# A one-core network of two mixing layers: order of stores, loads and projections in attention, and the values' rest on GpSimd

## The chip, the cores and the metric

The kernel runs on one core of a Trainium2 chip. The metric is the device time of one execution in microseconds, as the median of several executions. Engines are named as in the profile: PE is TensorE's matmul, PEld its weight load, DVE is VectorE, ACT is ScalarE, POOL is GpSimd, SP is SyncE, which here only issues DMAs.

## The reference, cut to what matters

Two layers on an input of 4 x 1024 x 256, each layer a mixing part and a feed-forward part with adaptive layer norms. The change touches only the second layer's attention:

```python
q = (h @ Wq).reshape(b, s, 16, 64).transpose(0, 2, 1, 3)
k = (h @ Wk).reshape(b, s, 4, 64).transpose(0, 2, 1, 3)
v = (h @ Wv).reshape(b, s, 4, 64).transpose(0, 2, 1, 3)
q, k = _apply_rope(q, cos, sin), _apply_rope(k, cos, sin)
scores = jnp.einsum('bkgqd,bkpd->bkgqp', q.reshape(b, 4, 4, s, 64), k) * scale
scores = jnp.where(causal, scores, -1e30)
out = jnp.einsum('bkgqp,bkpd->bkgqd', softmax(scores), v)
```

The rest is a long convolution by spectra, a feed-forward with binarized weights, and a mixture of two of eight experts.

## The kernel before

One loop of four turns, one for each batch element, runs on all engines; each engine's program is written out by hand in `before.py`, and semaphores tie them. A turn is: convolution part, feed-forward, attention (norm, projections, 16 heads), output projection, experts. float32 precision comes from splitting an operand into a high part (rounded to fp32r) and a low part (the rest), so a product costs three matmuls.

**Attention's opening.** `project(k, col)` on TensorE makes two blocks of 128 columns of queries or keys for one half of the 1024 rows: k = 0, 2 are the keys, 1, 3 the queries of heads 0 to 3, and 4 to 9 those of heads 4 to 15, two halves each. VectorE's `rotate(k)` multiplies each block by sine and cosine into `turned(k)`, a part of the tile `oT`; `rotate` on GpSimd (or `turn_and_add` on VectorE for k = 1, 3) adds them up; ScalarE's `high(k)` copies the high part, VectorE's `low(k)` subtracts for the low part (semaphore `rope_lo`). `project_values(h)` makes the values of one half; ScalarE's `value_rows(h)` copies their high part to `vhi` and VectorE's `value_low(h)` subtracts, from PSUM, into `vlo`. TensorE's order is: project 0, 1, values of half 0, norm, project 2, 3, the eight row scores of head 0 (`score_rows`), values of half 1, `turn_maxima(0)`, project 4, then the heads. All PSUM banks are handed out in turn by `Banks.take`; a taker waits for the last user of its bank.

**A head.** For head u the loop runs over 12 blocks n = 0 to 11 of (column half c, row tile j), `BLOCKS`. In each, TensorE makes the transposed scores of the block (`score_cols`: two matmuls, and on a diagonal block a third that adds the mask from `causal`), ScalarE takes the exponential twice (`exps`: full precision and high part), VectorE or GpSimd subtracts for the low part (`score_low`), and four blocks later TensorE multiplies with the values (`values`, three matmuls). The softmax's maxima come from a second set of scores, with query rows in partitions: `rows_at(u, n)` places the rows 0 to 3 of head u + 2 at blocks 8 to 11 and rows 4 to 7 of head u + 1 at blocks 0 to 3; VectorE reduces each (`row_maxima`). At block 6 the maxima of head u + 1 are turned over by TensorE (`turn_maxima`) and copied by ScalarE to `nmr`. Projections 5 to 9 stand at block 4 of heads 0, 3, 4, 7 and 8 (`PROJECT_AT`), their high and low parts at later blocks (`HIGH_AT`, `LOW_AT`). All have one buffer, `hrow`, so `high(k)` waits for the store of k - 1.

**SP's queue.** SP issues in order and waits in order. Its turn for head u (lines 1506 to 1534) waits for the exponentials of head u - 1, then loads the low queries of u + 1 (`load_query_low`) and the queries of u + 2 (`load_query`, tile `qhh`, three buffers) from the DRAM tensor `q_scratch`, at every fourth head the next keys, then the sums of head u - 1 (`load_sums`, 4 KB), the maxima of u + 1 (`load_maxima`), and the inverse of the sums through DRAM and back (`spread_inverse`, which waits for VectorE's reciprocal at block 9 and for its own store). Last, in heads 0, 1, 3, 4, 7 and 8 (`STORE_IN`), it waits for `rope_lo` and stores the turned queries of projection k, 1 MB, to `q_scratch`; where k is odd it then waits until both halves have landed.

TensorE's `score_rows(u, 0)` waits for `q_loaded(u)`, line 507 in the profile is its matmul.

Of the kernel before, what the change touches and what calls it, by code (L numbers as in the profile page):

```python
# [53 lines left out]
HIGH_AT = {(0, 7): 4, (1, 5): 5, (3, 9): 6, (4, 9): 7, (7, 9): 8, (8, 9): 9}  # L54
LOW_AT = {(0, 10): 4, (1, 8): 5, (3, 11): 6, (4, 11): 7, (7, 11): 8, (8, 11): 9}
STORE_IN = {0: 4, 1: 5, 3: 6, 4: 7, 7: 8, 8: 9}
# [55 lines left out]
def adaln_hyena_binffn_gqa_moe(nc, d, out, gate_scratch, kf_scratch, q_scratch, k_scratch, inverse_scratch, scratch):  # L112
    es = ExitStack()
    with es:
# [117 lines left out]
        def turned(k):  # L232

            n = k if k < 4 else 2 + k % 2
            return oT[:, 2 * n:2 * n + 2, :].rearrange("p a n -> p (a n)").rearrange("p (k n) -> p k n", n=HALF)
# [17 lines left out]
        def full(n):  # L253

            r = n % FRING
            return pT[:, r, :] if r < FRING - 1 else mix[:, 4:6, :].rearrange("p k n -> p (k n)")

        def stored_at(k):

            if k in (0, 2):  # L260
# [20 lines left out]
                 "m_loaded1", "v_high",  # L281
# [94 lines left out]
        def _(pe):  # L376
# [106 lines left out]
            def project_values(h):  # L483

                for t in range(4 * h, 4 * h + 4, 2):
                    b = bk.take(pe, ("v", t), until=(s["v_done"], t // 2 + 1))
# [124 lines left out]
            with pe.Fori(0, B):  # L611
# [43 lines left out]
                project(3, QCOL)  # L655
                for i in range(NT):
                    score_rows(0, i)
                project_values(1)
                turn_maxima(0)
                project(4, QCOL + GQ * HD)  # L660
# [66 lines left out]
        def _(act):  # L727
# [61 lines left out]
            def exps(u, c, j):  # L789
# [3 lines left out]
                if n == 0:  # L793
                    act.wait_ge(s["rest_stored0"], 16 * 2)
                    act.wait_ge(s["next_loaded"], 16 * 3)
                if n >= PRING:
# [30 lines left out]
            def value_rows(h):  # L827
                for t in range(4 * h, 4 * h + 4, 2):
                    b = bk.wait(act, ("v", t))
                    A(vhi[:, :, t:t + 2, 0:HD].rearrange("p g t n -> p t g n"),  # L830
                      ps[:, b, :].rearrange("p (t g n) -> p t g n", t=2, g=KV), ACT.Copy).then_inc(s["v_high"], 1)
# [7 lines left out]
            with act.Fori(0, B):  # L839
# [28 lines left out]
                for h in range(NHALF):  # L868
# [6 lines left out]
                    store_rest(2 * h + 1)  # L875
                value_rows(1)
                turn_maxima(0)
# [27 lines left out]
        def _(dve):  # L905
# [164 lines left out]
            def value_low(h):  # L1070

                for t in range(4 * h, 4 * h + 4, 2):
                    dve.wait_ge(s["v_high"], t // 2 + 1)
                    b = bk.wait(dve, ("v", t))
                    V.tensor_tensor(vlo[:, :, t:t + 2, 0:HD].rearrange("p g t n -> p t g n"),
                                    ps[:, b, :].rearrange("p (t g n) -> p t g n", t=2, g=KV),
                                    vhi[:, :, t:t + 2, 0:HD].rearrange("p g t n -> p t g n").bitcast(F32),
                                    ALU.subtract).then_inc(s["v_done"], 1)

# [28 lines left out]
            with dve.Fori(0, B) as bi:  # L1108
# [91 lines left out]
                value_low(0)  # L1200
# [3 lines left out]
                value_low(1)  # L1204
# [421 lines left out]
```

## Time and profile before

| | |
|---|---|
| median of 3 runs | 2111.86 us (2111.76 to 2113.53) |
| the profiled execution | 2106.92 us, span 2105.0 us |
| mean granted TensorE clock | 0.924 |
| PE busy | 1805.4 us, 86% |
| DVE busy | 1534.3 us, 73% |
| ACT busy | 987.6 us, 47% |
| POOL busy | 716.6 us, 34% |
| chain that ended last | PE 56%, DVE 19%, DMA 7%, issue 6% |

The profile is one execution on the chip. Times are microseconds from the start of the span. "Idle before" is the time an engine stood still before an instruction, with the one whose end released it. The granted clock is the share of the full 2.4 GHz at which TensorE was let run: 1.00 or, at the lower of its two levels, 0.50; a stretch that holds both has a mean between. Attention's 16 heads lie between about 262 and 516 us in the first turn, and again in each of the other three.

### The profile page before, as it was taken

Reading aid. Unit: us, or ns where it says so; the run is one execution under the profiler, and the core shown is the slowest. Engines: PE = TensorE matmul, PEld = TensorE weight load, DVE = VectorE, ACT = ScalarE, POOL = GpSimd, SP = SyncE. Lnnn points to the kernel's source line nnn. Section 1 sums busy time; section 2 is a strip of 40 time slices with the busy share of each in tenths; the row PEclk is TensorE's granted clock in tenths of the full one; section 3 lists DMA queues with packets and bytes.
Section 4 is the critical chain, followed back from the end, with each engine's and each line's share of the span. In section 5 each row is a group of like instructions: output and inputs, shape, how many; then the busy total and the mean of one; then the engine's idle time right before and its main releaser. Section 6 shows DMA issues by size and latency. Waiting matters only on the chain.

```text
span 2105.0 us, 27381 instructions
## 1 busy us (share of the span) xinstructions
PE 1805.4 (86%) x9108; PEld 1451.2 (69%) x9108; DVE 1534.3 (73%) x2774; ACT 987.6 (47%) x2113; POOL 716.6 (34%) x747
## 2 busy tenths in 40 slices
PE   6868799999875889999977778999987687999997
PEld 3747677778764767778765567777776576777885
DVE  4588878875658887777448887777654978778745
ACT  1303266776320446667431326667722033666742
POOL 0051144533224234444115214444411513444321
PEclk8988899999987989999989889999998898999998
DMA  6500334431410053443150034433241004344305
GB/s 237 191 1 1 104 101 112 106 87 47 180 51 1 1 149 101 103 116 72 32 215 0 1 82 114 116 96 86 52 180 62 0 1 120 96 116 117 81 27 200
DMA packets 92184, 187.14 MB, mean 89 GB/s; under 512 B 29119, under 2 KB 44287, under 8 KB 88326
## 3 DMA queue, kind: packets, MB, share of 16 engines
q1 hardware_dynamic: 84742, 171.66, 27.9%
q10 hardware_dynamic: 7296, 13.63, 2.3%
q8 instruction: 80, 1.31, 0.3%
q14 instruction: 66, 0.54, 0.1%
HBM read 129.39 MB, written 45.89 MB: 83 GB/s over the span
## 4 chain that ended last, share of the span: by engine, by line
PE 56%; DVE 19%; DMA 7%; issue 6%; DVEq 5%; ACT 3%; POOL 2%; SPq 1%; POOLq 1%; ACTq 0%
PE ps L384 8%; PE ps L507 6%; PE ps L679 5%; PE ps L527 5%; PE ps L550 5%; PE ps L547 5%; PE ps L548 5%; PE ps L529 5%; PE ps L390 3%; PE ps L720 3%; DMA qhh<-q_scratch 2%; DVE hrow L978 2%; DMA q_scratch<-hrow 2%; DVE psplit L1083 2%; DVE ps L1063 2%
## 5 line engine op out<-in xcount | busy, mean ns | idle before, releaser
L1308 POOL TENSOR_TENSOR psplit<-pT,psplit 128x384 fp32r<-128x384 f32 (+3 forms) x320 | 303.7, 961 | 547.2 <-ACT psplit L801 543.7
L1063 DVE CUSTOM_DVE_ANT_0 ps<-ps,mrow 128x128 f32<-128x128 f32 (+7 forms) x512 | 385.3, 766 | 132.8 <-PE ps L507 131.8
L801 ACT ACTIVATE psplit<-ps 128x512 fp32r<-128x512 f32 (+3 forms) x768 | 373.0, 486 | 0.0
L800 ACT ACTIVATE pT<-ps 128x512 f32<-128x512 f32 (+3 forms) x512 | 256.5, 501 | 214.4 <-PE ps L533 135.4
L507 PE MATMUL ps<-khl,qhh 128*128 128x512 f32 (+3 forms) x768 | 253.0, 392 | 76.0 <-DMA qhh<-q_scratch 26.3
L527 PE MATMUL ps<-qhh,khl 128*128 128x512 f32 (+3 forms) x768 | 272.8, 355 | 0.4
L529 PE MATMUL ps<-q,k 65*128 65x512 f32 (+3 forms) x768 | 269.3, 351 | 0.0
L547 PE MATMUL ps<-psplit,vhi 128*65 128x512 f32 (+3 forms) x768 | 267.9, 349 | 0.0
L550 PE MATMUL ps<-psplit,vhi 128*65 128x512 f32 (+3 forms) x768 | 262.9, 342 | 0.0
L548 PE MATMUL ps<-psplit,vlo 128*65 128x512 f32 (+3 forms) x768 | 262.3, 341 | 0.0
L759 ACT ACTIVATE work<-ps,modb 128x512 f32<-128x512 f32 x48 | 37.3, 777 | 400.6 <-PE ps L462 400.6
L507 PEld LDWEIGHTS ps<-khl,qhh 128*128 128x128 f32 x768 | 132.4, 201 | 99.3 <-issue 51.4
L527 PEld LDWEIGHTS ps<-qhh,khl 128*128 128x128 f32 x768 | 146.7, 191 | 51.6 <-DVE mx L1063 4.9
L1275 POOL TENSOR_TENSOR rstd<-var,neghalf 128x4 f32<-128x4 f32 x34 | 34.5, 1015 | 430.3 <-DVE var L975 430.3
L1083 DVE TENSOR_TENSOR psplit<-pT,psplit 128x512 fp32r<-128x512 f32 x192 | 131.2, 708 | 48.7 <-ACT psplit L801 47.9
L529 PEld LDWEIGHTS ps<-q,k 65*128 65x128 f32 x768 | 147.1, 192 | 17.4
L800 ACT ACTIVATE mix<-ps 128x512 f32<-128x512 f32 (+2 forms) x256 | 117.9, 461 | 84.3 <-PE ps L529 49.9
L384 PE MATMUL ps<-hT,wqkv 128*128 128x512 f32 x480 | 127.9, 422 | 19.0 <-DVE hT L987 19.0
L550 PEld LDWEIGHTS ps<-psplit,vhi 128*65 128x65 f32 x768 | 106.0, 138 | 44.3 <-issue 3.0
L1083 DVE TENSOR_TENSOR psplit<-mix,psplit 128x512 fp32r<-128x512 f32 x128 | 99.2, 775 | 42.8 <-ACT psplit L801 42.8
L548 PEld LDWEIGHTS ps<-psplit,vlo 128*65 128x65 f32 x768 | 106.2, 138 | 34.8
L1094 DVE TENSOR_TENSOR oT<-work,mix 64x1024 f32<-64x1024 f32 x64 | 94.3, 1474 | 45.5 <-DMA mix<-inverse_scratch 44.6
(176 smaller groups left out, 3505.7 us busy)
## 6 DMA issues: line engine op xcount, KB each, us to landing
qhh<-q_scratch SPq DMA_DIRECT2D x112, 256.0 KB, 4.9
q_scratch<-hrow SPq DMA_DIRECT2D x24, 1024.0 KB, 5.4
mix<-inverse_scratch SPq DMA_DIRECT2D x64, 256.0 KB, 3.5
q<-q_scratch SPq DMA_DIRECT2D x56, 256.0 KB, 4.3
sgn<-sgn_scratch SPq DMA_DIRECT2D x8, 1024.0 KB, 13.3
Kf<-kf_scratch SPq DMA_DIRECT2D x4, 2048.0 KB, 17.5
khl<-k_scratch SPq DMA_DIRECT2D x24, 256.0 KB, 6.5
in_w<-in_w_scratch SPq DMA_DIRECT2D x4, 1536.0 KB, 10.5
```

Of the source, the lines that this page charges most:

```text
L384: i = mm(o, lhs(a, q), rhs(c, q), start=n == 0, stop=n == len(pairs) - 1)
L507: q = mm(ps[:, b + c // HALF, 0:e - c], qhh[:, r, i * P:(i + 1) * P], khl[:, g % 2, c:e], start=True, stop=True)
L527: mm(ps[:, b, 0:hi - lo], khl[:, g % 2, j * P:(j + 1) * P], qhh[:, r, lo:hi], start=True, stop=False)
L529: i = mm(ps[:, b, 0:hi - lo], k2[:, g % 2, j * P:(j + 1) * P], q2[:, u % 2, lo:hi], start=False, stop=not diagonal)
L547: mm(o, vhi[:, g, j, :], high, start=j == 0, stop=False)
L548: mm(o, vlo[:, g, j, :], high, start=False, stop=False)
L550: mm(o, vhi[:, g, j, :], low, start=False, stop=j == 4 * c + 3).then_inc(s["pv_done"], 1)
L800: A(full(n)[:, 0:hi - lo], ps[:, b, 0:hi - lo], ACT.Exp, scale=SCALE)
L801: A(psplit[:, n % PRING, 0, 0:hi - lo], ps[:, b, 0:hi - lo], ACT.Exp, scale=SCALE)\
L1063: V.tensor_tensor_reduce(out=v, in0=v, in1=mrow[:, L - n:L], scale=1.0, scalar=-3e38, op0=ALU.add, op1=ALU.max, accum_out=mx[:, u % 2, i:i ...
L1083: V.tensor_tensor(psplit[:, n % PRING, 1, 0:m], full(n)[:, 0:m], psplit[:, n % PRING, 0, 0:m].bitcast(F32), ALU.subtract)\
L1308: G.tensor_tensor(psplit[:, n % PRING, 1, 0:m], full(n)[:, 0:m], psplit[:, n % PRING, 0, 0:m].bitcast(F32), ALU.subtract)\
```

## The change

- SP: the loads of head u's turn are no longer behind the wait for the store's landing. Stores 6 to 9 go right behind `load_query` in heads 4, 5, 8 and 9 (`STORE_FIRST`); stores 4 and 5 stay at the end of heads 0 and 1 (`STORE_LATE`) without a wait behind them. The wait for both halves stands ahead of the `load_query` that is the first to read them, in heads 2, 6 and 10.
- High and low parts of projections 4 and 5 come at earlier blocks.
- TensorE: project 4 goes ahead of head 0's row scores, `turn_maxima(0)` ahead of the values of half 1. `turned(4)` lies where `turned(1)` was.
- Values: ScalarE copies them twice, the high part and all of it (`vfull`, in room of `pT` and `oT`); GpSimd subtracts. The bank is free after ScalarE's copies. The first two exponentials wait for GpSimd, as they write that room. VectorE's `value_low` is gone, and rotates 4 where it stood.
- ScalarE: the values of half 1 come behind the copy of head 0's maxima. GpSimd: `rotate(0)` comes ahead of its fills, then the values' low parts of half 0, `rotate(2)`, `rotate(4)`, the low parts of half 1.

```diff
-HIGH_AT = {(0, 7): 4, (1, 5): 5, (3, 9): 6, (4, 9): 7, (7, 9): 8, (8, 9): 9}
-LOW_AT = {(0, 10): 4, (1, 8): 5, (3, 11): 6, (4, 11): 7, (7, 11): 8, (8, 11): 9}
-STORE_IN = {0: 4, 1: 5, 3: 6, 4: 7, 7: 8, 8: 9}
+HIGH_AT = {(0, 4): 4, (1, 2): 5, (3, 9): 6, (4, 9): 7, (7, 9): 8, (8, 9): 9}
+LOW_AT = {(0, 6): 4, (1, 5): 5, (3, 11): 6, (4, 11): 7, (7, 11): 8, (8, 11): 9}
+STORE_LATE = {0: 4, 1: 5}
+STORE_FIRST = {4: 6, 5: 7, 8: 8, 9: 9}
...
-            n = k if k < 4 else 2 + k % 2
+            n = k if k < 4 else 1 if k == 4 else 2 + k % 2
...
+        def vfull(t):
+
+            return pT[:, t // 2, :] if t < 4 else oT[:, 0, (t - 4) * D:(t - 2) * D]
...
                 project(2, KCOL)
                 project(3, QCOL)
+                project(4, QCOL + GQ * HD)
                 for i in range(NT):
                     score_rows(0, i)
+                turn_maxima(0)
                 project_values(1)
-                turn_maxima(0)
-                project(4, QCOL + GQ * HD)
...
+                if n < 2:
+                    act.wait_ge(s["v_done"], n + 1)
...
-                      ps[:, b, :].rearrange("p (t g n) -> p t g n", t=2, g=KV), ACT.Copy).then_inc(s["v_high"], 1)
+                      ps[:, b, :].rearrange("p (t g n) -> p t g n", t=2, g=KV), ACT.Copy)
+                    A(vfull(t), ps[:, b, :], ACT.Copy).then_inc(s["v_copied"], 1)
...
+                turn_maxima(0)
+                act.wait_ge(s["rope_lo"], 1)
                 value_rows(1)
-                turn_maxima(0)
...
-                value_low(0)
+                rotate(4)
                 for i in range(NT):
                     row_maxima(0, i)
                 negate(0)
-                value_low(1)
-                rotate(4)
...
+            def value_low(h):
+
+                for t in range(4 * h, 4 * h + 4, 2):
+                    pool.wait_ge(s["v_copied"], t // 2 + 1)
+                    G.tensor_tensor(vlo[:, :, t:t + 2, 0:HD].rearrange("p g t n -> p t g n"),
+                                    vfull(t).rearrange("p (t g n) -> p t g n", t=2, g=KV),
+                                    vhi[:, :, t:t + 2, 0:HD].rearrange("p g t n -> p t g n").bitcast(F32),
+                                    ALU.subtract).then_inc(s["v_done"], 1)
...
+                rotate(0)
                 G.memset(vhi[:, :, :, HD:HD + 1].bitcast(F32), 1.0)
...
-                for k in (0, 2):
-                    rotate(k)
+                value_low(0)
+                rotate(2)
+                rotate(4)
+                value_low(1)
...
                     if u + 2 < HEADS:
+                        if u and (u + 2) % GQ == 0:
+                            for k in (2 * g + 4, 2 * g + 5):
+                                sp.wait_ge(*rope_stored(k))
                         load_query(u + 2)
+                    if u in STORE_FIRST:
+                        store(STORE_FIRST[u])
...
-                    if u in STORE_IN:
-                        store(STORE_IN[u])
-                        if STORE_IN[u] % 2:
-                            for k in (STORE_IN[u] - 1, STORE_IN[u]):
-                                sp.wait_ge(*rope_stored(k))
+                    if u in STORE_LATE:
+                        store(STORE_LATE[u])
```

## Rows read from the trace of the kernel before

**Rows 1.** Windows between copies of the maxima: length, busy by engine, clock, DMA.

```profile
core 0: us, PE busy (x) PEld busy (x) DVE busy (x) ACT busy (x) POOL busy (x), PEclk, DMA share, GB/s
303.68:325.46 21.78, 18.39 (x94) 14.53 (x93) 13.50 (x26) 11.21 (x29) 7.47 (x9) 0.92 0.34 76
342.99:357.95 14.96, 14.49 (x85) 11.45 (x84) 13.44 (x27) 11.88 (x30) 8.25 (x8) 1.00 0.46 137
357.95:376.71 18.76, 15.79 (x83) 12.23 (x81) 11.29 (x25) 11.02 (x28) 5.64 (x7) 0.91 0.36 82
376.71:393.32 16.61, 16.61 (x94) 13.29 (x93) 13.20 (x26) 10.94 (x29) 7.37 (x9) 1.00 0.28 65
425.91:443.09 17.18, 14.25 (x83) 11.22 (x82) 11.29 (x25) 11.03 (x29) 5.61 (x7) 1.00 0.41 87
443.09:457.14 14.05, 14.05 (x83) 11.22 (x82) 10.76 (x25) 10.76 (x28) 5.57 (x7) 1.00 0.34 77
928.76:947.46 18.70, 15.85 (x83) 12.52 (x82) 11.29 (x25) 11.03 (x28) 5.64 (x7) 0.91 0.36 81
1815.74:1837.41 21.67, 18.41 (x94) 14.53 (x93) 13.49 (x26) 11.21 (x29) 7.48 (x9) 0.92 0.32 75
1869.98:1888.81 18.83, 15.80 (x83) 12.27 (x82) 11.30 (x25) 11.03 (x29) 5.61 (x7) 0.91 0.35 82
1938.01:1955.20 17.19, 14.26 (x83) 11.22 (x82) 11.29 (x25) 11.03 (x29) 5.62 (x7) 1.00 0.41 89
```

**Rows 2.** Timeline from 348 to 362: start, duration, engine, line, operation, idle before.

```profile
348.72 0.31 ACT L801 ACTIVATE psplit<-ps 128x128 fp32r<-128x128 f32 x1
...
349.52 0.49 SPq L1494 DMA_DIRECT2D mix<-inverse_scratch  x1
...
350.62 0.58 SPq L1454 DMA_DIRECT2D q_scratch<-hrow  x1
...
355.41 0.53 SPq L1473 DMA_DIRECT2D q<-q_scratch  x1
...
355.99 1.24 SPq L1468 DMA_DIRECT2D qhh<-q_scratch  x2
...
361.35 0.30 PE L507 MATMUL ps<-khl,qhh 128*128 128x128 f32 x1 [2.97 <-DMA qhh<-q_scratch]
```

**Rows 3.** Timeline from 290 to 312, heads 1 and 2.

```profile
292.30 1.22 DVE L1056 TENSOR_TENSOR hrow<-oT,hrow 128x1024 fp32r<-128x1024 f32 x1
...
295.94 0.60 SPq L1454 DMA_DIRECT2D q_scratch<-hrow  x1
...
302.06 1.24 SPq L1468 DMA_DIRECT2D qhh<-q_scratch  x2
...
307.55 0.30 PE L507 MATMUL ps<-khl,qhh 128*128 128x128 f32 x1 [3.39 <-issue]
```

**Rows 4.** Timeline from 248 to 263, attention's opening.

```profile
248.21 1.93 PE L507 MATMUL ps<-khl,qhh 128*128 128x128 f32 x4 [5.75 <-DVE vlo L1075]
...
254.11 4.27 PE L384 MATMUL ps<-wqkv,hT 128*128 128x256 f32 x24
...
256.13 0.17 DVE L1068 TENSOR_SCALAR nm<-mx 128x8 f32<-128x8 f32 x1
...
258.24 3.05 PE L384 MATMUL ps<-hT,wqkv 128*128 128x512 f32 x12
...
259.18 1.28 ACT L800 ACT_TABLE_LOAD   x1
259.93 1.22 DVE L1042 TENSOR_TENSOR oT<-ps,rope 128x1024 f32<-128x1024 f32 x1 [0.18 <-PE ps L384]
...
262.04 0.60 ACT L800 ACTIVATE pT<-ps 128x512 f32<-128x512 f32 x1 [1.58 <-PE ps L533]
```

**Rows 5.** Groups by form, 262 to 516: count, busy us, mean ns, idle before.

```profile
L1056 DVE TENSOR_TENSOR hrow<-oT,hrow 128x1024 fp32r<-128x1024 f32 x6 | 8.7, 1457 | 0.0
...
L1308 POOL TENSOR_TENSOR psplit<-pT,psplit 128x512 fp32r<-128x512 f32 x16 | 20.7, 1291 | 32.0 <-ACT psplit L801 32.0
```

**Rows 6.** Loads of the sums, tile `den`: from issue to landing, all 64.

```profile
DMA to landing us min/median/max: 1.9/2.0/7.5
```

More of the change, by code:

```diff
@@ L280, in adaln_hyena_binffn_gqa_moe @@
                  "q_loaded1", "q_loaded2", "q2_loaded0", "q2_loaded1", "k_loaded0", "k_loaded1", "v_done", "nm_done", "nmr_done", "m_loaded0",
-                 "m_loaded1", "v_high",
+                 "m_loaded1", "v_copied",
                  "exp_done", "causal_made", "low_pool", "low_dve", "pv_done", "o_done", "sum_loaded", "inverse_done",
@@ L485, in project_values @@
                 for t in range(4 * h, 4 * h + 4, 2):
-                    b = bk.take(pe, ("v", t), until=(s["v_done"], t // 2 + 1))
+                    b = bk.take(pe, ("v", t), until=(s["v_copied"], t // 2 + 1))
                     for u in range(2):
@@ L1068, in negate @@
                 V.tensor_scalar(nm[:, u % 2, :], mx[:, u % 2, :], -1.0, None, ALU.mult).then_inc(s["nm_done"], 1)
[L1070 to L1078, printed above, removed]
             def score_low(u, c, j):
@@ L1367, in _ @@
                             score_low(u, c, j)
-                        if (u, n) == (0, 3):
-                            rotate(4)
                         if (u, n) in PROJECT_AT:
```

## The prediction

> **What bounds the kernel now.** I read the windows of attention first, cut from one copy of the negated row maxima to the next (the copy stands at block 6 of each head), so that each stretch is one head's length. A head at its best takes 14.05 us and TensorE is busy in all of it, VectorE for 10.76, ScalarE for 10.76, GpSimd for 5.57 [rows 1]. A head that also carries one query projection takes 16.61, again with TensorE busy throughout. So attention is bound by TensorE, and whatever makes TensorE idle is paid in full. The next thing to look for is which heads are longer than 14.05 or 16.61. Three a batch are much longer: the stretch of 21.78 (one projection in it), the one of 18.76, and the one of 17.18 to 18.94 [rows 1]. In all three the timeline shows TensorE standing still for about 3 us before the first row score of a head two ahead, and ended by the landing of that head's queries [rows 2, 3]. In most of them the granted clock of the stretch is then 0.91 or 0.92 instead of 1.00, with TensorE busy 15.79 us for work that takes 14.05 elsewhere [rows 1]: the stall also costs a piece at the lower level. Last comes the opening, read in the timeline.
>
> **Loads of queries no longer behind the store, heads 5 and 9.** Before, SP issues the store of turned queries at 350.62, waits for it to land, and only at 355.41 and 355.99 issues the loads of head 6's low parts and head 7's queries; TensorE waits 2.97 us for the latter, until 361.35 [rows 2]. The last exponential of head 4 starts at 348.72 and SP is through with the inverse at 349.52 + 0.49, so in the changed order the low load goes at about 350.1, the queries at 350.7, and the store behind them at about 352. They took at most 361.35 - 355.99 = 5.36 us to arrive; from 350.7 that is 356.1, and TensorE asks for them at 361.35 - 2.97 = 358.4. The stall goes, with 2.3 us to spare. What is late next is nothing: VectorE had 11.29 us of work in that stretch. Worth, against 14.05: the stretch of head 5 is 18.76 in the first batch and 18.83 in the fourth (four such, the two between read 19.02 and 18.81), 19.2 us in all; that of head 9 is 17.18, 18.70, 18.94 and 17.19, 15.8 us in all [rows 1]. Sum **-35.0**. Bounds: all of it, or -28 if each of the eight stretches stays 0.9 us long, as the one from 342.99 is.
>
> **Head 2.** Here the load of head 4's queries needs the store of k = 5 itself, so the wait stays; it only moves behind the low load. Before: low part made at 292.30 (1.22 us), store 295.94, loads 302.06, TensorE waits 3.39 until 307.55 [rows 3]. After: that low part is made at block 5 instead of 8, where VectorE has room, so the reciprocal, the inverse's store and its load, on which SP is blocked ahead of this store, come about 0.9 earlier; and the low load of 0.54 is no longer ahead of the queries' load. That makes the load some 1.6 us earlier and its flight perhaps 0.4 shorter. The stall falls from 3.4 to about 1.4. Whether the clock then stays up has no row for a gap of that length in this place; the stretch from 342.99, whose waits are short, stays at 1.00, those of head 2 at 0.92 [rows 1]. The stretch exceeds 16.61 by 5.17 to 5.06 (first and fourth batch, of four; 20.8 us in all). Of each I take 2.0 of stall and 1.7 of the clock, **-14.8**. Bounds: -2.4 (only 0.6 a batch and a clock as before) and -20.8.
>
> **Store behind the loads, heads 4 and 8.** The store issued just ahead of head 6's and 10's loads now follows them. The stretch of 14.96 us is 0.9 over a clean head [rows 1]; of that I take the part which is waiting for queries, 0.7 for the two heads of a batch, **-2.7**. Bounds: 0 and -7.5.
>
> **The opening.** Three moves at once. Project 4 (12 matmuls, 3.05 us) leaves the place between the maxima and head 0 and goes ahead of the first row scores, where TensorE idles: they began at 248.21 after 5.75 us of waiting [rows 4]. Worth nothing there, as the scores of the second four rows wait for a DMA that does not come earlier. The values' 24 matmuls (4.27 us) had lain beside VectorE's maxima; they now follow the turned maxima and lie beside the maxima's own DMA. So 4.27 in place of 3.05 stands behind the negation of 256.13. VectorE gains and loses about equally ahead of it (the low values' two subtractions out, two rotations of 1.22 in, partly beside waiting): +0.4. ScalarE makes two copies per pair of tiles rather than one (four more a batch, 0.60 each as I take them from an exponential of the same shape), and those of the last two pairs come behind the maxima's copy, and the table load of 1.28 behind them. Followed step by step: negation 256.5, values end about 261.5, copies 262.6, table load 263.9, first exponential 263.9 in place of 262.04. The first row score of head 1 waits for the same copies and comes at 262.6, as before. The third block of head 0 takes the bank that the first pair of exponentials (two of 0.60) frees, at about 265.1 in place of 263.2, and the row scores behind it wait. I take +1.5 a batch, **+6.0**; bounds -4 (the values run at full clock and ScalarE's extra copies hide) and +12. The values of the first half cost ScalarE two more copies ahead of the norm's second half, some 0.3 us, inside that. GpSimd's four subtractions at about 1.29 each take the place of VectorE's; they end near 264.4, before the first low part is asked for, so nothing. The waits of the first two exponentials on them are long met.
>
> On the table load the trace has 1.28 us and its engine idle after it [rows 4]. The Trainium skill (ScalarE: Activation LUTs, What ACT_TABLE_LOAD costs) counts a drain of about the same length on top, 2.66 us in all. That speaks against the change: by it the first exponential would come another 1.4 us later and the sum be about 5.5 us worse. No row shows the drain.
>
> **The sum.** -35.0 - 14.8 - 2.7 + 6.0 = -46.5. The profiled execution took 2106.92 (span 2105.0), the timed runs have their median at 2111.86, so 4.9 us above it, about what two or three more stretches at the lower clock make. I set the change on the median: 2111.86 - 46.5 = **2065.4** (2060.4 on the profiled one's footing).
>
> **The rivals.**
> A, *small gain*: head 2 keeps its stall and its low clock (-2.4) and the opening costs its bound (+12). With -35 for heads 5 and 9 and -1 for heads 4 and 8 that is -26: 2085. For it: store and load in series remain. Against: the wait shrinks by SP's order alone.
> B, *GpSimd in VectorE's way*: the subtractions of the first values (two of 1.29) fall beside VectorE's own low parts of the first half, which have two operands in SBUF. That form takes 1.22 where GpSimd is still and has a mean of 1.46 over six in attention [rows 3, 5]. Priced at two blocked lengths, 2.6, less the 1.25 VectorE waits for TensorE just after, it is +1.3 a batch: 2071. The Trainium skill (SBUF - State Buffer, on the shared port pair) says that the second of two such operations waits for the whole first one; the mean of 1.46 agrees in part. It lies inside the range.
> C, *slower than before*: the 1 MB store, now issued behind the loads, lies ahead of the 4 KB row of sums. That row lands in 2.0 us at the median but 7.5 at worst [rows 6]. Issued some 5 us into the head, about 355.6, and landing 7.5 later, it would be there at 363.1, while VectorE asks for it near 359.2; VectorE, in order, holds the row maxima behind its reciprocal, TensorE stands 3.9 us and loses another 1.6 at the lower clock. At four heads of four batches that is 16 x 5.5 = 88 against 46.5 won: 2153. It decides the sign once it costs over 2.9 us a head. Against: the store had landed 4.8 us after its issue [rows 2], so from 352 it is done at about 357.
> D, *it does not do what it says*: the query loads are held by something else (the exponentials of the head before), the stall of heads 5 and 9 stays by two thirds; -12 - 5 + 6: 2101. Against: the exponential at 348.72.
>
> **How the numbers follow.** Forecast with B inside it 0.68 (2050 to 2078), A 0.18, D 0.05, C 0.03, a gain above the forecast's own range 0.06. The range for 8 in 10 goes from 2050 to 2086: it takes in the forecast and most of A. About 0.2% (4.2 us) is what a measurement of this kernel can tell from no change: faster 0.94 (all but C and some of D), same 0.02 and slower 0.04 (C, and D with the opening at its bound).
>
> **What would show it.** The stretches of heads 5 and 9 at 14.05 to 14.3 with the clock at 1.00; the query load of head 7 issued before the store; the one of head 2 near 18 to 19; heads 4 and 8 at 14.3 to 14.7; the first exponential 1 to 3 us later after the negation than 5.9. It is wrong if a stretch of heads 5 or 9 stays above 16, if VectorE waits at the reciprocal, or if TensorE stands still ahead of head 0's third block for over 3 us.

## The result, and the profile after

| | before | after |
|---|---|---|
| median | 2112.63 us (2111.76 to 2113.53, 4 runs) | 2074.87 us (2071.98 to 2080.39, 4 runs) |
| the profiled execution | 2106.92, span 2105.0 | 2071.98, span 2070.2 |
| chain that ended last | PE 56%, DVE 19%, DMA 7% | PE 61%, DVE 17%, DMA 2% |

The ratio is 0.9824, interval [0.9802, 0.9847]: 37.8 us faster on the medians, 34.8 on the spans of the profiled executions. The forecast was 2065.4, with 2050 to 2086 around it. The direction held and the time is in the range; of the 46.5 us forecast, about 35 to 38 came. The profiled execution of after is the fastest of its four runs, and what is read from its trace is that one's.

I cut the trace of every kernel in the same way. The marks of a turn are VectorE's first normalised row of attention's norm, the negation of head 0's maxima, and ScalarE's copies of the maxima of head 1, 2 and so on, which delimit the heads as in [rows 1]. A stretch has the name of the head in whose block 6 it begins, so head 2's, the 21.78 of [rows 1], runs from the copy of head 3's maxima to that of head 4's. The one called "head 1", here and in the expectations, is an exception: it is the stretch from the copy of head 1's maxima to that of head 2's, from block 6 of head 0 to block 6 of head 1. What lies between two marks is compared turn by turn. Means over the four turns, in us; the last line is what one turn of after differs from before:

| | norm row to negation | negation to copy of head 1's maxima | "head 1" | head 2 | head 5 | head 9 |
|---|---|---|---|---|---|---|
| before | 31.23 | 17.76 | 15.45 | 21.81 | 18.86 | 18.00 |
| after | 33.22 | 18.99 | 14.44 | 19.61 | 14.05 | 14.07 |
| difference | +1.99 | +1.23 | -1.01 | -2.20 | -4.81 | -3.93 |

The other heads agree within 0.1. Times four that is +8.0 +4.9 -4.0 -8.8 -19.2 -15.7 = -34.8, which is the whole of what the spans differ by: outside attention both kernels spend 1004.2 to 1004.3 us.

The windows of after. Columns: stretch and its length, busy time of each engine (instructions), TensorE's granted clock, DMA share, GB/s. The first is head 2 in the first turn, the second head 2 in the second turn, then heads 4, 5 and 9 of the first:

```profile
307.09:327.21 20.12, 18.40 (x94) 14.41 (x93) 13.50 (x26) 11.22 (x29) 7.50 (x9) 0.92 0.26 63
802.04:820.35 18.31, 16.84 (x94) 13.27 (x93) 13.50 (x26) 11.21 (x28) 7.46 (x9) 1.00 0.30 65
344.74:359.79 15.05, 14.83 (x85) 11.46 (x84) 13.14 (x27) 11.67 (x30) 8.70 (x8) 1.00 0.55 143
359.79:373.85 14.06, 14.06 (x83) 11.22 (x82) 11.02 (x25) 10.79 (x29) 5.56 (x7) 1.00 0.37 87
423.05:437.12 14.07, 14.07 (x83) 11.20 (x82) 11.02 (x25) 10.78 (x28) 5.58 (x7) 1.00 0.39 85
```

Where [rows 1] had 18.76 for head 5 and 17.18 to 18.94 for head 9, there is now a clean head: TensorE busy all of it, clock 1.00. SP's queue around it, in the timeline (start, duration):

```profile
351.83 0.60 SPq L1480 DMA_DIRECT2D q<-q_scratch  x1
352.47 1.24 SPq L1475 DMA_DIRECT2D qhh<-q_scratch  x2
353.75 0.60 SPq L1461 DMA_DIRECT2D q_scratch<-hrow  x1
358.02 0.51 SPq L1491 DMA_DIRECT2D den<-work  x1
```

The two loads are issued first and the store behind them; in [rows 2] the store came first and the loads 4.8 us after it. Head 2, in contrast, still has a stall and, in three turns of four, still loses clock: TensorE is busy 18.40 in the first line above for the work that takes it 16.84 in the second.

### The profile page after: what moved, and what is told of

Its sections match the earlier page's. It is cut to its first block, busy times and chain, and to the rows that moved or that the text cites. A ratio compares the mean times of both kernels' runs of the same rounds, so it can differ in the third digit from the quotient of the medians.

```text
span 2070.2 us, 27393 instructions
## 1 busy us (share of the span) xinstructions
PE 1795.0 (87%) x9108; PEld 1441.8 (70%) x9108; DVE 1520.4 (73%) x2758; ACT 994.4 (48%) x2129; POOL 735.9 (36%) x763
## 4 chain that ended last, share of the span: by engine, by line
PE 61%; DVE 17%; ACT 5%; DVEq 5%; issue 5%; POOL 3%; DMA 2%; ACTq 1%; SPq 1%; POOLq 0%
PE ps L389 8%; PE ps L512 7%; PE ps L532 6%; PE ps L534 6%; PE ps L555 5%; PE ps L552 5%; PE ps L553 5%; PE ps L684 5%; PE ps L395 5%; PE ps L725 3%; DMA gate_scratch<-grow 2%; DVE prod L1140 2%; PE ps L538 2%; DVE ps L1072 1%; DVE oT L1093 1%
## 5 line engine op out<-in xcount | busy, mean ns | idle before, releaser
L552 PE MATMUL ps<-psplit,vhi 128*65 128x512 f32 (+3 forms) x768 | 265.2, 345 | 0.0
L555 PE MATMUL ps<-psplit,vhi 128*65 128x512 f32 (+3 forms) x768 | 259.7, 338 | 0.0
L389 PEld LDWEIGHTS ps<-hT,wqkv 128*128 128x128 f32 x480 | 98.0, 206 | 48.6 <-DVE hT L996 24.7
## 6 DMA issues: line engine op xcount, KB each, us to landing
Kf<-kf_scratch SPq DMA_DIRECT2D x4, 2048.0 KB, 17.5
```

The source lines that it names most:

```text
L389: i = mm(o, lhs(a, q), rhs(c, q), start=n == 0, stop=n == len(pairs) - 1)
L552: mm(o, vhi[:, g, j, :], high, start=j == 0, stop=False)
L555: mm(o, vhi[:, g, j, :], low, start=False, stop=j == 4 * c + 3).then_inc(s["pv_done"], 1)
```

## The experiments

A time is the median of the kernel's runs, and the ratio is to the kernel before, measured beside it on the same chip. Two kernels have one run each and no interval. Each stretch below is read from one profiled execution, of four turns.

### SP's order alone

The kernel before, with only SP's order changed as in the change:

```diff
-STORE_IN = {0: 4, 1: 5, 3: 6, 4: 7, 7: 8, 8: 9}
+STORE_LATE = {0: 4, 1: 5}
+STORE_FIRST = {4: 6, 5: 7, 8: 8, 9: 9}
...
+                        if u and (u + 2) % GQ == 0:
+                            for k in (2 * g + 4, 2 * g + 5):
+                                sp.wait_ge(*rope_stored(k))
...
+                    if u in STORE_FIRST:
+                        store(STORE_FIRST[u])
```

> The kernel before with SP's new order alone (stores behind the loads, the wait for landing ahead of the load that needs it); opening, high and low parts as before. Theory 1 (SP's order is the whole gain, the opening costs about 5 us net): the stretches of heads 5 and 9 fall to 14.05 (35 us), head 2's stretch of 21.8 loses about 0.6 us a batch; heads 0 and 1 keep 15.13 and 15.45; 2074 to 2077. Rival (the gain needs the earlier parts or the other opening too): heads 5 or 9 stay above 16, 2085 or more.

Measured: 2070.62 (2065.89 to 2072.47), ratio 0.9796 [0.978, 0.9812], below the 2074 to 2077 expected. Heads 5 and 9 are 14.05 and 14.07 in the mean, as in after. "Head 1" is as before (15.44), head 2 only a little shorter (20.91 for 21.81). So the part of the change that touches SP alone is worth all that the whole change is, on fewer edits: the opening and the earlier parts together add nothing. The windows of "head 1" and head 2 in the first turn:

```profile
275.77:291.20 15.43, 14.96 (x86) 11.58 (x84) 12.72 (x24) 12.53 (x30) 7.99 (x8) 1.00 0.45 121
305.31:325.98 20.67, 18.45 (x94) 14.38 (x93) 13.51 (x26) 11.21 (x29) 7.47 (x9) 0.92 0.29 71
```

### The same with the earlier high and low parts

```diff
-HIGH_AT = {(0, 7): 4, (1, 5): 5, (3, 9): 6, (4, 9): 7, (7, 9): 8, (8, 9): 9}
-LOW_AT = {(0, 10): 4, (1, 8): 5, (3, 11): 6, (4, 11): 7, (7, 11): 8, (8, 11): 9}
+HIGH_AT = {(0, 4): 4, (1, 2): 5, (3, 9): 6, (4, 9): 7, (7, 9): 8, (8, 9): 9}
+LOW_AT = {(0, 6): 4, (1, 5): 5, (3, 11): 6, (4, 11): 7, (7, 11): 8, (8, 11): 9}
```

> The same plus the earlier high and low parts of projections 4 and 5; the opening as before. Theory 1: head 2's stretch falls from about 21.2 to 18.3 to 20.1 as in the changed kernel, and head 1's from 15.45 to 14.43; with the opening's 13 us (8 ahead of the negation, 5 behind it) left out, 2061 to 2064. Rival (the 14.43 comes from the opening's order, not from the earlier parts): head 1 stays at 15.45 and the time is 2066 to 2069.

Measured: 2056.45 (2054.2 to 2058.27), ratio 0.9733 [0.9716, 0.9749], again below what was expected. Against the kernel above that is another 14.2 us. The same two windows:

```profile
275.51:289.95 14.44, 14.44 (x84) 11.45 (x83) 12.72 (x25) 11.75 (x29) 7.86 (x8) 1.00 0.44 129
304.04:322.59 18.55, 16.87 (x94) 13.28 (x93) 13.50 (x26) 11.23 (x28) 7.46 (x9) 1.00 0.29 69
```

"Head 1" loses 0.5 us of TensorE's idle time and 0.5 of its busy time, 1.0 in every turn. Head 2 keeps 1.3 to 1.7 us of idle time, but the clock stays at 1.00, in all four turns (18.12 to 18.55). That is the second half of what head 2 was forecast to bring. In after, with the same order of SP and the same blocks, three turns of four lose it again.

### The opening alone

The change's opening (projections' order, two copies on ScalarE, low values and rotations on GpSimd), with SP's order and the parts' blocks as before:

```diff
-            n = k if k < 4 else 2 + k % 2
+            n = k if k < 4 else 1 if k == 4 else 2 + k % 2
...
                 project_values(1)
-                project(4, QCOL + GQ * HD)
...
-                value_low(1)
-                rotate(4)
```

> The changed kernel with SP's old order and the old places of the high and low parts: the opening's change alone (project 4 first, maxima before values, values' low parts on GpSimd). Theory 1: it costs 2.0 us a batch from the norm to the negation and 0.3 to 3.5 behind it, 2122 to 2127. Rival (the opening gains or costs nothing by itself, and the loss seen came from the earlier high and low parts): 2110 to 2115.

Measured: 2133.15 (2133.0 to 2135.18), ratio 1.01 [1.0084, 1.0117]: **slower than before by 20.8 us**. From norm row to negation it takes 33.12 (31.23 before), from there to the copy of head 1's maxima 21.17 (17.76), and head 2 22.71 (21.81). The first two of these make (1.89 + 3.41) x 4 = 21.2; the rest adds 3, head 2 +3.6 and head 9 +4.2 (19.06 for 18.00) against head 5's -4.7 (17.69 for 18.86), where the old stalls stand and the clock fell in other turns than before. The expectation, 2122 to 2127, was too low. So the opening is a loss, over three times what I had put for it.

### Store 5 earlier still

The kernel with SP's order and the earlier parts, and in head 1 the store of k = 5 ahead of the inverse of the sums (for whose reciprocal SP otherwise waits first):

```diff
-STORE_LATE = {0: 4, 1: 5}
+STORE_LATE = {0: 4}
...
                         load_maxima(u + 1)
...
+                    if u == 1:
+                        store(5)
                     if u:
                         spread_inverse(u - 1)
```

> As the second, with the store of projection 5 moved ahead of the inverse's two DMAs in SP's queue, so that it is issued at block 6 of head 1 instead of 9. Theory 1 (head 2's rest of 1.5 us of stall and 1.8 of clock is only the queue's order): its stretch falls to 16.6 to 16.9, 2050 to 2054. Rival (the 1 MB store slows the 4 KB rows of sums and inverse that now follow it, and VectorE stands at the reciprocal): heads 1 and 2 grow by 1 us or more, no gain over the second.

Measured: 2046.96 (2045.96 to 2050.86), ratio 0.9695 [0.9678, 0.9711]. This is the fastest of the kernels with several runs, 27.9 us below after on the medians, and the intervals of the two ratios are far apart. Head 2 is at the 16.6 of any head with a projection, in all four turns (16.66 to 16.67):

```profile
301.22:317.88 16.66, 16.66 (x94) 13.24 (x93) 13.20 (x26) 10.95 (x28) 7.40 (x9) 1.00 0.29 65
```

The low part of k = 5 and its store, first in the kernel without this edit, then with it (first turn of each):

```profile
289.76 1.22 DVE L1057 TENSOR_TENSOR hrow<-oT,hrow 128x1024 fp32r<-128x1024 f32 x1
295.44 0.60 SPq L1455 DMA_DIRECT2D q_scratch<-hrow  x1
```

```profile
286.95 1.22 DVE L1057 TENSOR_TENSOR hrow<-oT,hrow 128x1024 fp32r<-128x1024 f32 x1
288.19 0.57 SPq L1455 DMA_DIRECT2D q_scratch<-hrow  x1
```

The store goes 4.5 us after the low part has ended in the first and 0.02 after it in the second. So what was left of head 2's stall was SP, blocked at the wait for the reciprocal (which VectorE makes at 293.26 in the first) and at the inverse's own store, while `rope_lo` of k = 5 had long been reached.

### The low values of half 0 behind a rotation

The first of two experiments on the opening of after. It asks whether GpSimd's two subtractions beside VectorE are what lengthens the part up to the negation:

```diff
                 rotate(0)
-                value_low(0)
                 rotate(2)
+                value_low(0)
```

> The changed kernel with GpSimd's subtractions for the first half's values moved behind its rotation of the second half's keys, so that they no longer run beside VectorE's low part of the norm (1.72 us there, 0.69 alone). Theory (the clash of VectorE and GpSimd is 1.2 to 1.5 of the 2.0 us that the stretch from the norm's rows to the negation grew, ScalarE's two copies the rest): that stretch falls from 33.2 to 31.9; 2068 to 2071. Rival (ScalarE's copies alone delay it): 33.0 or more, 2074 to 2076.

Measured: 2076.81 (2073.47 to 2079.09), ratio 0.9837 [0.982, 0.9853]: the same as after, a miss against 2068 to 2071. Up to the negation it takes 32.30 and 32.31 in two turns, but 32.99 and 33.01 in the others, so 0.6 shorter in the mean; behind it the part grows from 18.99 to 20.64. The timeline of the first turn shows why, in the values' matmuls that follow the negation (4.45 us, where after has 3.07; in the other turns 4.43, 5.47 and 5.47):

```profile
256.65 0.27 PE L519 MATMUL ps<-identr,nm 128*8 128x128 f32 x1 [2.14 <-DVE nm L1077]
256.68 4.45 PE L389 MATMUL ps<-wqkv,hT 128*128 128x256 f32 x24
```

A gain of 0.2 to 0.9 ahead of the negation was taken back by the clock behind it. As a test of GpSimd's place the run is inconclusive by itself.

### A table load in ScalarE's wait

After, with one dummy exponential of one element ahead of the copy of head 0's maxima, so that the exponential's table is loaded while ScalarE waits (nothing of the computation is left out; the written element is overwritten):

```diff
             def body_act():
...
+                A(nmr[0:1, 1, 0:1], ident[0:1, 0:1], ACT.Exp)
                 turn_maxima(0)
                 act.wait_ge(s["rope_lo"], 1)
                 value_rows(1)
```

> The changed kernel with one exponential of a single element on ScalarE ahead of the copy of the maxima, so that the table is loaded in ScalarE's wait and not behind the values' copies. Theory (the table load behind the copies holds the first exponential, and by its bank head 0's third block, for 1.02 us): the first exponential comes 1.1 to 1.3 us earlier after the negation (4.6 in place of 5.85) and the copy of head 1's maxima 0.6 to 1.0 earlier; 2070 to 2073. Rival (the row maxima of head 1 on VectorE set that stretch anyway): no more than 0.2 a batch, 2074 to 2076.

Measured: 2060.75 (2055.89 to 2064.23), ratio 0.975 [0.9729, 0.9772], 14 us below after and more than the 2070 to 2073 expected. The timeline of the third turn:

```profile
1245.42 1.28 ACT L884 ACT_TABLE_LOAD   x1 [9.91 <-issue]
1245.97 0.17 DVE L1078 TENSOR_SCALAR nm<-mx 128x8 f32<-128x8 f32 x1
1249.92 0.59 ACT L839 ACTIVATE oT<-ps 128x512 f32<-128x512 f32 x1
1250.39 0.61 ACT L807 ACTIVATE pT<-ps 128x512 f32<-128x512 f32 x1
```

The load ends at 1246.70, just before ScalarE's copy of the turned maxima at 1246.82 and well ahead of the values' copies, and the first exponential follows the last copy directly, 4.42 us after the negation rather than 5.85. In the three other turns the values' matmuls ran wholly or partly at the lower clock. Where they took 5.47 us in both kernels, the exponential came at 6.82 against 8.25. So at either clock the load is worth 1.43 us to the first exponential, and the stretch up to the copy of head 1's maxima is 2.1 us shorter at the full clock (16.03 for 18.14 to 18.19) and 3.0 at the lower one (18.41 and 18.43 for 21.44). The whole 14 us can't be put down to it: in the two traces, 8.5 us apart, the opening gives 5.6, as three turns here ran their matmuls below the full clock and one of after did, and 3.1 come from head 2, which kept its clock in three turns of four.

### The values on GpSimd alone, and its parts

Three kernels on the fastest one (SP's order, earlier parts, early store 5), all with the old order of projections. The first moves the low values to GpSimd, with ScalarE's second copy:

```diff
-                      ps[:, b, :].rearrange("p (t g n) -> p t g n", t=2, g=KV), ACT.Copy).then_inc(s["v_high"], 1)
+                      ps[:, b, :].rearrange("p (t g n) -> p t g n", t=2, g=KV), ACT.Copy)
+                    A(vfull(t), ps[:, b, :], ACT.Copy).then_inc(s["v_copied"], 1)
...
-                value_low(0)
...
-                value_low(1)
...
-                for k in (0, 2):
-                    rotate(k)
+                rotate(0)
+                value_low(0)
+                rotate(2)
+                value_low(1)
```

> The fastest so far (stores behind loads, earlier parts, store 5 ahead of the inverse) with the values' low parts on GpSimd and ScalarE's second copy, but the old order of projections. Theory (the 2.0 us ahead of the negation come from this part of the change, not from the order): norm to negation 33.0 to 33.3 in place of 31.3, the rest as there; 2052 to 2056. Rival (they come from project 4 and its rotation ahead of the row scores): 31.0 to 31.6, 2044 to 2048.

Measured: 2055.55 (2052.94 to 2057.92), ratio 0.9728 [0.9712, 0.9744], slower than the fastest by 8.6 us. The time is as expected. Up to the negation it takes 32.91 (31.33 in the fastest kernel); behind it 17.55 (17.70).

The second has ScalarE's second copy alone (and the wait for `rope_lo` that its room needs), whose result is not read; VectorE subtracts from PSUM as before:

```diff
-                      ps[:, b, :].rearrange("p (t g n) -> p t g n", t=2, g=KV), ACT.Copy).then_inc(s["v_high"], 1)
+                      ps[:, b, :].rearrange("p (t g n) -> p t g n", t=2, g=KV), ACT.Copy)
+                    A(vfull(t), ps[:, b, :], ACT.Copy).then_inc(s["v_high"], 1)
```

> sp_early5 with ScalarE's second copy of the values alone; VectorE still makes their low parts from PSUM, and nothing reads the copy. Theory: of the 1.6 us from the norm to the negation that gp_values showed over sp_early5, these copies are 0.5 (31.8 in place of 31.3), the rest is GpSimd beside VectorE. Rival (the copies are all of it): 32.7 or more.

Measured: one run, 2046.21. Up to the negation 31.41: the copies cost 0.1 a turn, not the expected 0.5. So 1.5 of the 1.6 belongs to the subtractions on GpSimd.

The third is the first with `value_low(0)` behind `rotate(2)`:

> gp_values with GpSimd's subtractions for the first half moved behind its rotation of the second half's keys, out of the way of VectorE's low part of the norm. Theory (the clash is about 1 us of the 1.6): norm to negation 31.8 to 32.1 in place of 32.9. Rival (no clash, only copies): 32.7 or more.

Measured: one run, 2046.47; norm row to negation 33.01, 33.00, 32.30 and 32.96, where 31.8 to 32.1 was expected. It hardly fell (32.81 in the mean for 32.91); the collision only moved to the next pair of operations of VectorE. The timeline of the first turn:

```profile
243.17 2.77 POOL L1319 TENSOR_TENSOR vlo<-pT,vhi 128x512 fp32r<-128x512 f32 x2
243.74 1.17 DVE L1058 TENSOR_TENSOR oT<-oT 128x512 f32<-128x512 f32 x1
244.83 1.67 DVE L1059 TENSOR_TENSOR oT<-oT 128x512 f32<-128x512 f32 x1
```

The same two operations alone take 0.69 and 0.68, a few microseconds earlier in that trace:

```profile
233.90 0.69 DVE L1058 TENSOR_TENSOR oT<-oT 128x512 f32<-128x512 f32 x1
234.51 0.68 DVE L1059 TENSOR_TENSOR oT<-oT 128x512 f32<-128x512 f32 x1
```

A VectorE operation with an operand in PSUM was not lengthened beside GpSimd (1.23 us here, where the mean of nine is 1.22); in between, in the same trace:

```profile
240.69 1.30 POOL L1312 TENSOR_TENSOR oT<-oT 128x512 f32<-128x512 f32 x1 [8.24 <-DVE oT L1051]
241.02 1.23 DVE L1051 TENSOR_TENSOR oT<-ps,rope 128x1024 f32<-128x1024 f32 x1 [0.41 <-PE ps L389]
```

That this one run is as short as the fastest kernel's is not a gain of the part: behind the negation it is 17.04 for 17.70, the sum of both parts still 0.8 a turn longer, and the 3.6 us that made it up lie outside attention (1000.0 for 1003.6), where the two kernels have the same instructions.

### The old place of the values, with the rest of the opening

After, with store 5 early, `value_low(0)` behind `rotate(2)`, and the values of half 1 back ahead of the turn of the maxima on TensorE and ScalarE:

```diff
-                turn_maxima(0)
                 project_values(1)
+                turn_maxima(0)
```

> The changed kernel with store 5 ahead of the inverse, GpSimd's subtractions moved as in the first of these, and the values of the second half back beside the row maxima, ahead of the turned maxima, on TensorE and ScalarE; project 4 stays ahead of the row scores. Theory (what the new order costs is the values' place: 24 matmuls alone behind the negation, at the lower clock in some turns; project 4's place is free): norm to negation 31.9, negation to head 1's copy 16.5 to 17.6 in every turn; 2043 to 2047. Rival (TensorE's long pause ahead of the second row scores sets the clock anyway, and project 4's place brings it): over 17.9, 2050 or more.

Measured: 2054.18 (2051.75 to 2056.88), ratio 0.973 [0.9714, 0.9746]. From the negation to head 1's maxima it takes 17.50 to 17.52 in every turn, where after has 18.14 to 21.45 and the opening alone 20.03 to 21.58. Ahead of it nothing is won (32.85, where 31.9 was expected), and the time misses the 2043 to 2047 expected. The values beside VectorE's maxima are so out of the way, and the clock at which they run stops mattering.

### Heads 4, 5, 8 and 9

The fastest kernel with the high and low parts of k = 6 to 9 at blocks 2 and 5 of the next head, as those of k = 5 are, and their stores at the same place:

```diff
-HIGH_AT = {(0, 4): 4, (1, 2): 5, (3, 9): 6, (4, 9): 7, (7, 9): 8, (8, 9): 9}
-LOW_AT = {(0, 6): 4, (1, 5): 5, (3, 11): 6, (4, 11): 7, (7, 11): 8, (8, 11): 9}
-STORE_FIRST = {4: 6, 5: 7, 8: 8, 9: 9}
+HIGH_AT = {(0, 4): 4, (1, 2): 5, (4, 2): 6, (5, 2): 7, (8, 2): 8, (9, 2): 9}
+LOW_AT = {(0, 6): 4, (1, 5): 5, (4, 5): 6, (5, 5): 7, (8, 5): 8, (9, 5): 9}
+STORE_MID = {1: 5, 4: 6, 5: 7, 8: 8, 9: 9}
...
                         load_maxima(u + 1)
-                    if u == 1:
-                        store(5)
+                    if u in STORE_MID:
+                        store(STORE_MID[u])
```

> The fastest so far (sp_early5) with high and low parts of projections 6 to 9 moved from blocks 9 and 11 to blocks 2 and 5 of the next head, and their stores between the load of the maxima and the inverse in heads 4, 5, 8 and 9. Theory (the 0.9 to 1.0 us by which four heads still exceed 16.61 and 14.05 is the low part on VectorE at block 11, ahead of four long row maxima that TensorE's banks wait for, as head 1's extra 1.0 was the low part at block 8): the stretches of 17.55 and 15.05 fall to 16.6 and 14.1, 15 us in all; 2030 to 2034. Rival (the excess belongs to the DMAs of the keys and the store): they stay, 2045 to 2048.

Measured: 2049.05 (2047.01 to 2050.51), ratio 0.9704 [0.9684, 0.9723]: no gain, a miss. The windows of heads 3 and 4:

```profile
319.42:336.48 17.06, 17.06 (x96) 13.52 (x95) 14.73 (x27) 12.03 (x30) 9.14 (x10) 1.00 0.51 109
336.48:352.01 15.53, 14.71 (x85) 11.39 (x84) 13.38 (x27) 11.85 (x29) 7.34 (x8) 1.00 0.49 137
```

Head 3 is 0.5 shorter, head 4 0.5 longer, head 5 0.18 longer (14.22 in the mean); heads 7 and 8 do as 3 and 4, and head 10 is 0.4 longer (14.46). What is over a clean head moved and did not shrink, though the four low parts took VectorE 1.21 to 1.23 here and up to 1.49 before. What it is made of stays open. The parallel that the expectation drew doesn't hold either: in the trace of before the low part at block 8 of head 1 starts at 292.30 [rows 3], behind the stretch that became 1.0 shorter, which ends at 289.49; the low part inside that stretch is that of k = 4.

## Why the prediction was right, and where its size was off

**Heads 5 and 9: right, to the size.** -35.0 was forecast; the table gives (4.81 + 3.93) x 4 = 35.0. The steps were as described: SP is no longer blocked, the loads go first. They go at 351.83 and 352.47. The stretch of head 4 begins at 344.74 here and at 342.99 in [rows 1], 1.75 earlier; less that, the loads are at 350.08 and 350.72, where the forecast had 350.1 and 350.7. That SP's order alone does it is shown by the kernel with SP's order alone.

**Head 2: right mechanism, size too large by 6.** Forecast 3.7 a turn, -14.8 in all; measured 2.20, -8.8. The first half held: the stall fell from over 3 us to 1.47 to 1.72, where 1.4 was forecast; in the first turn of after:

```profile
309.27 0.30 PE L512 MATMUL ps<-khl,qhh 128*128 128x128 f32 x1 [1.72 <-ACT psplit L808]
```

The profile names ScalarE as what released it. But the load of these queries, issued at 304.92, lands at 309.19, 0.08 us before, and in the kernel with the early store 5 the wait is gone: it was for the queries. The second half failed: "of each I take 1.7 of the clock". It was there in one turn of four (18.31), in the kernel with SP's order and the earlier parts in all four. The stall's length doesn't tell them apart: in after the turns with 1.53, 1.68 and 1.72 lost the clock and the one with 1.47 kept it, in the other kernel one with 1.68 kept it. Two more kernels with the same code there (the low values behind the rotation, the early table load) kept it in three turns of four each. What decides which turn keeps the clock was not found; the choice to take the clock as regained, with no row for a gap of that length, is the step that failed. Store 5 ahead of the inverse shows what the forecast had named and not followed: the reciprocal on which SP is blocked.

**"Head 1": missed.** The forecast saw in the earlier parts of k = 4 and 5 only a help for head 2. They are worth 1.0 a turn in this stretch as well, -4.0 in all: 15.44 with SP's order alone, 14.44 with them. Before, the low part of k = 4 came at block 10 of head 0, beside two of GpSimd's subtractions, and took 1.88 to 1.89 in every turn:

```profile
278.44 2.70 POOL L1308 TENSOR_TENSOR psplit<-pT,psplit 128x384 fp32r<-128x384 f32 x2 [2.86 <-ACT psplit L801]
278.65 1.89 DVE L1056 TENSOR_TENSOR hrow<-oT,hrow 128x1024 fp32r<-128x1024 f32 x1
```

At block 6, where GpSimd has no low part to make, it takes 1.21 in every turn of after. So the row that prices rival B, 0.7 us for one operation, was in the trace of before; how much of the 1.0 it explains wasn't separated. The 1.22 of [rows 3] that the forecast took as one beside a still GpSimd had a subtraction of GpSimd's beginning 0.64 into it, at 292.94, which then took 1.45.

**Heads 4 and 8: wrong by 2.7.** 15.05 and 15.04 after, 15.02 and 15.02 before: the store's place among the loads gives nothing there. The step that failed was to read 0.7 of the 0.9 over a clean head as waiting for queries. In the window of head 4 of after, TensorE is idle for only 0.22 of the 15.05 and busy for 14.83, which is 0.77 over the 14.06 of head 5. Of what kind that extra busy time is stays open.

**The opening: direction right, size wrong, +12.9 for +6.0** in the traces of before and after; +20.8 as the kernel with the opening alone has it, and +18.4 as after stands above the kernel that lacks only the opening. In the traces 8.0 of the 12.9 lie ahead of the negation, where +0.4 a turn, 1.6, was forecast, and 4.9 behind it, for the other 4.4: the term that was mis-sized is the first.

Ahead of the negation it is +1.99 a turn, where VectorE's balance was put at +0.4. Rival B is the cause, in a larger size. Its +1.3 stood beside the forecast as a case of its own; it belonged in the sum. The kernels of the values put it at 1.5 (32.91 less 31.41), which with the copies' 0.1 and the forecast's 0.4 makes the 1.99; that these 0.4 are project 4 and its rotation wasn't tested by itself. The timeline of after has it in full:

```profile
235.66 2.79 POOL L1319 TENSOR_TENSOR vlo<-pT,vhi 128x512 fp32r<-128x512 f32 x2
235.68 1.72 DVE L996 TENSOR_TENSOR hT<-work,hT 128x512 fp32r<-128x512 f32 x1 [0.65 <-ACT hT L765]
237.49 1.50 DVE L1058 TENSOR_TENSOR oT<-oT 128x512 f32<-128x512 f32 x1
238.92 0.68 DVE L1059 TENSOR_TENSOR oT<-oT 128x512 f32<-128x512 f32 x1
```

While GpSimd runs its two subtractions (235.66 to 238.45), VectorE's operations of two SBUF operands take 1.72 and 1.50; just behind them the like of the second takes 0.68. That is 1.0 and 0.8 more, 1.8 in all, and both stand on the path: TensorE's next projection waits for the first (4.73 us idle before it, ended by `hT`, where before has 3.49). The victims were not the low parts of the first half that the forecast named but the low part of the norm's second half (L996) and the rotation's additions. GpSimd's own operations, which began first, hardly suffer (2.79 for two, against 1.29 each in [rows 5]). The Trainium skill (SBUF — State Buffer, on the shared port pair) has the second of two such operations wait for the whole first one. The runs agree in who waits, and less in how long: a subtraction of that pair takes 1.39, GpSimd's first began 0.02 ahead of VectorE's operation, and VectorE's two operations lost 1.03 and 0.82.

Behind the negation the steps came as forecast: values, two copies for each pair, table load, first exponential, and head 0's third block waiting for the exponentials. The timeline of after, first turn:

```profile
260.39 0.17 DVE L1077 TENSOR_SCALAR nm<-mx 128x8 f32<-128x8 f32 x1
260.73 3.07 PE L389 MATMUL ps<-wqkv,hT 128*128 128x256 f32 x24
264.34 0.58 ACT L839 ACTIVATE oT<-ps 128x512 f32<-128x512 f32 x1
264.94 1.28 ACT L807 ACT_TABLE_LOAD   x1
266.24 0.60 ACT L807 ACTIVATE pT<-ps 128x512 f32<-128x512 f32 x1
267.37 0.39 PE L532 MATMUL ps<-qhh,khl 128*128 128x256 f32 x1 [1.02 <-ACT psplit L808]
```

But the 24 matmuls have two lengths in after, not the one of 4.27 that I took from before. In three turns of after they run at full clock, 3.07, and the first exponential is at +5.85, as early as before (5.39 to 5.91), +0.4 to the copy of head 1's maxima (18.14 to 18.19 for 17.76). In the fourth they take 5.47 and the copy comes 3.3 later:

```profile
260.70:263.80 3.10, 3.10 (x25) 2.90 (x25) 0.00 (x0) 1.35 (x3) 0.15 (x1) 1.00 0.69 174
1741.97:1747.44 5.47, 5.47 (x26) 5.47 (x27) 0.00 (x0) 1.35 (x3) 1.19 (x1) 0.51 0.60 148
```

Both follow a pause of 2.14 us ahead of the maxima's turn. In the kernel with the opening alone the copy of head 1's maxima is at +20.0 to +21.6 in all four turns. Placed behind a stretch in which TensorE mostly waits, the values are at the mercy of the clock; placed beside the maxima (the last but one kernel) their clock is hidden and the part is 17.5 in every turn. So the forecast's +1.1 a turn for this part (its +1.5 less the +0.4) is about the mean of what after shows (+1.23), and 2.3 less than what the opening alone shows (+3.41). That it is so near is luck: no turn has it, three have +0.4 and one +3.7. Why after got the full clock three times of four, and the same opening elsewhere not, is open.

The forecast weighed a drain behind the table load, by the Trainium skill (ScalarE: Activation LUTs, What ACT_TABLE_LOAD costs), at 1.4 us. The traces do not show it: the load ends at 264.94 + 1.28 = 266.22 and the exponential starts at 266.24; in the third turn of the kernel with the early load, it ends at 1246.70 and ScalarE's next instruction starts at 1246.71.

**Rivals.** A did not come as drawn (head 2 did move, by more than its -2.4), but its opening at +12 did: 2085 and the forecast's 2065.4 have the result between them, about as far from either. B came, and its 2071 is the nearest of all, though at +1.5 a turn and on other operations of VectorE than it named. C did not come: TensorE is busy throughout the windows of heads 5 and 9, and VectorE never stands still before a reciprocal. One figure of the forecast's case against it was off, though: behind the loads the stores 6 to 9 took 7.0 to 8.5 us to land and not 4.8. The row of sums issued behind one at 358.02 landed at 361.47, 1.9 us ahead of the reciprocal at 363.33. D is excluded by the same windows.

**The ledger**, in us: forecast -35.0 -14.8 -2.7 +6.0 = -46.5; found -35.0 -8.8 -4.0 ("head 1") 0 +12.9 = -34.9. So one large term carries the forecast. Three smaller ones came out 6.0, 2.7 and 6.9 worse than put, and only the missed term gave 4.0 back; that the time is still in the range owes something to that, and to the opening costing 12.9 in after and not the 20.8 of the kernel that has it alone.

## What to carry to other kernels

When a queue that issues in order also waits in order, look first at what stands behind each wait: moving two loads ahead of a wait was worth 35 us, and moving one store ahead of another wait 9 more, with no work saved. Then look at what lands later for it: here a row of sums kept 1.9 us of slack. Handing an elementwise operation to GpSimd isn't free for VectorE even where GpSimd is idle: beside it VectorE's own operations of two SBUF operands took 1.2 to 1.7 us for 0.7, and 1.9 for 1.2, so place it where VectorE waits or, as far as the one row here shows, works from PSUM. Don't put a block of matmuls on the path right behind a stretch in which TensorE mostly idles: it may run at either clock, and the same block where something else is awaited cost nothing here.

## What the runs showed that I had not expected

- The clock behind short stalls differs between turns of one execution and between kernels whose code there is the same. Head 2 with a stall of 1.3 to 1.7 us kept 1.00 in all four turns of one kernel and in one of four of after; in after a stall of 1.53 lost it, and elsewhere one of 1.80 kept it. 24 equal matmuls behind an equal pause of 2.14 us took 3.07, 5.47 or something between. Without the stall head 2 read 16.65 to 16.68 in every turn of six kernels.
- VectorE's operations of two SBUF operands were held up over the length of GpSimd's pair in both of its places: 1.5 and 1.4 us a turn more than with the copies alone (32.91 and 32.81 for 31.41).
- The first normalised row of attention in the first turn comes at 224.0 to 228.0 us in the profiled executions of kernels with the same instructions up to there. So some 4 us of the differences between single executions lie outside what was changed.
